# Sums of two attention masks moved from VectorE to GpSimd, two tiles ahead of their use

## What is computed

```python
qp = einsum(q, Wq) + bq ; kp = einsum(k, Wk) + bk
scores = qp @ kp.T * H ** -0.5 * layernorm(x)          # qc_score
mask = attn_mask[None, :, :] | key_padding_mask[:, None, :]
scores = where(mask, -inf, scores)
x = x + tanh(g_xattn) * softmax(scores)
h = layernorm(x)
logits = h @ gate_w.T ; w, sel = top_k(softmax(logits), 8)
x = x + tanh(g_ffn) * moe(h, sel, w, wg, wu, wd)
```

## Time and profile before

| | us |
|---|---|
| median of 3 runs | 1843.42 (1843.0 to 1848.21) |
| the profiled execution, its own time | 1842.44 |
| its span, from first to last instruction | 1840.7 |
| busy: PE, DVE, ACT, POOL | 1797.5, 1450.3, 1236.2, 1064.7 |

### The profile page before, as it was taken

How to read it: one execution, slowest core, us unless ns; L and a number is a source line. 1 busy time by engine, 2 the same in 40 slices (tenths; PEclk the granted TensorE clock), 3 DMA queues, 4 the chain that set the end, 5 groups by cost and what they waited for, 6 DMA issues and landing times.

```text
span 1840.7 us, 37183 instructions
## 1 busy us (share of the span) xinstructions
PE 1797.5 (98%) x13149; PEld 1316.9 (72%) x13149; DVE 1450.3 (79%) x2523; ACT 1236.2 (67%) x1806; POOL 1064.7 (58%) x817
## 2 busy tenths in 40 slices
PE   9999986999999999999999999999999999999997
PEld 4666655777777777777777777777777777777775
DVE  5999998777777777777777777777777777777772
ACT  6999986566666666666666666666666666666662
POOL 1000002776667666666666666677667766666651
PEclk9999997999999999999999999999999999999999
DMA  8677753799989999999999999999999999999982
GB/s 257 217 247 267 240 209 147 267 324 300 301 283 313 300 298 299 300 299 299 302 302 304 304 305 306 303 305 306 307 302 301 297 300 299 299 299 298 299 285 46
DMA packets 93849, 516.98 MB, mean 281 GB/s; under 512 B 17136, under 2 KB 19696, under 8 KB 69872
## 3 DMA queue, kind: packets, MB, share of 16 engines
q1 hardware_dynamic: 47056, 357.19, 49.3%
q0 software_dynamic: 43008, 151.04, 34.7%
q10 hardware_dynamic: 3744, 8.26, 1.6%
HBM read 409.21 MB, written 107.22 MB: 281 GB/s over the span
## 4 chain that ended last, share of the span: by engine, by line
PE 89%; DVE 5%; issue 2%; DMA 2%; ACT 1%; SPq 0%; POOL 0%; POOLq 0%; DVEq 0%; ACTq 0%
PE ps_gu L531 54%; PE ps_d L540 27%; PE ps_s L412 4%; PE ps_l L432 2%; PE ps_j L401 2%; DMA xb<-in_x 1%; DVE zb L898 1%; DVE zb L870 1%; PE ps_t L424 1%; DMA xg<-h_rows,g_idx 1%; DVE at L932 1%; PE ps_w L447 0%; DVE at L940 0%; ACT hT L645 0%; DVE hrow L960 0%
## 5 line engine op out<-in xcount | busy, mean ns | idle before, releaser
L1304 POOL DMA_INDIRECT xg<-h_rows,g_idx x504 | 724.5, 1437 | 187.9 <-issue 132.4
L531 PE MATMUL ps_gu<-xT,split_g 128*128 128x256 bf16 x4608 | 534.4, 273 | 0.7 <-DVE xT L1186 0.7
L531 PE MATMUL ps_gu<-xT,split_u 128*128 128x256 bf16 x4608 | 534.4, 273 | 0.0
L540 PE MATMUL ps_d<-split_d,act 128*128 128x512 bf16 x2304 | 507.9, 379 | 0.4 <-DVE act L1138 0.4
L531 PEld LDWEIGHTS ps_gu<-xT,split_g 128*128 128x128 bf16 x4608 | 450.8, 98 | 66.5 <-issue 0.9
L531 PEld LDWEIGHTS ps_gu<-xT,split_u 128*128 128x128 bf16 x4608 | 450.9, 98 | 52.2
L540 PEld LDWEIGHTS ps_d<-split_d,act 128*128 128x128 bf16 x2304 | 225.3, 98 | 259.1 <-DVE act L1138 1.2
L783 ACT ACTIVATE ob<-ps_d,wcol 128x512 f32<-128x512 f32 x256 | 173.1, 688 | 338.3 <-PE ps_d L540 338.3
L1324 POOL DMA_INDIRECT out<-ob,s_idx x128 | 205.4, 1604 | 294.2 <-ACT ob L783 202.5
L1146 DVE STREAM_TRANSPOSE xt<-xg 128x512 f32<-128x512 f32 x252 | 163.9, 689 | 151.2 <-DMA xg<-h_rows,g_idx 151.2
L1128 DVE TENSOR_TENSOR split_d<-raw_d,split_d 128x1536 bf16<-128x1536 f32 x128 | 219.3, 1753 | 73.1 <-ACT split_d L755 73.1
(11 more groups left out here) (116 smaller groups left out, 1402.3 us busy)
## 6 DMA issues: line engine op xcount, KB each, us to landing
raw_d<-in_wd SPq DMA_DIRECT2D x63, 1536.0 KB
raw_g<-in_wg SPq DMA_DIRECT2D x62, 1536.0 KB
raw_u<-in_wu SPq DMA_DIRECT2D x62, 1536.0 KB, 16.0
h_rows<-hrow SPq DMA_DIRECT2D x34, 640.0 KB, 3.4
xb<-in_x SPq DMA_DIRECT2D x32, 512.0 KB, 4.4
out<-xb SPq DMA_DIRECT2D x32, 512.0 KB, 3.2
xg<-h_rows,g_idx POOLq DMA_INDIRECT x512, 3.3
ctx_sb<-in_ctxT SPq DMA_DIRECT2D x8, 512.0 KB, 6.0
```

Source lines behind the costliest of these rows:

```text
L531: mm = pe.matmul(ps_gu[m][:, t, :], w[:, wi, k, m * P:(m + 1) * P], xT[u][:, k, xi, :], start=(k == 0 and (wi, xi) == (0, 0)), stop=(k == ...
L540: mm = pe.matmul(ps_d[n][:], act[u][:, ai, m, half * P:(half + 1) * P], split_d[:, wi, m, c * NH:(c + 1) * NH], start=(m == 0 and (wi, ai) ...
L1304: p.indirect_dma_start(out=xg[u][:, g, :], out_offset=None, in_=h_rows, in_offset=bass.IndirectOffsetOnAxis(ap=g_idx[u][:, g:g + 1].bitcas ...
```

## The change

`both` leaves VectorE's order and is issued by GpSimd. `both(0)`, `both(1)`, `both(2)` stand there behind the two first powers, and `both(g + 3)` behind `inverse_root(g)`. It waits for the pieces of the mask, for `kpm_used`, and for the `row_max` that last read its buffer (`z_ready`). The key mask's conversion stays on VectorE, where it now waits for the last sum of the batch before (`both_made`).

```diff
-            def both(g):
-
-                if g % TB == 0 and g:
-                    key_mask(g // TB)
-                v.wait_ge(kpm_used, g // TB + 1)
-                v.tensor_tensor(both_add[:, g % 2], mask_add[:, g % TB], kpm_add[:], ALU.add).then_inc(both_made, 1)
...
             v.wait_ge(mask_used, 2)
-            both(0)
-            both(1)
             minus_mean(1)
...
-            both(2)
...
                 step(picks, g - 1)
-                if g + 3 < N:
-                    both(g + 3)
+                if (g + 3) % TB == 0 and g + 3 < N:
+                    v.wait_ge(both_made, g + 3)
+                    key_mask((g + 3) // TB)
                 step(picks, g - 1)
                 minus_mean1(g)
...
+            def both(g):
+
+                p.wait_ge(mask_used, min(g % TB + 1, 2) if g < 2 else TB)
+                p.wait_ge(kpm_used, g // TB + 1)
+                if g >= 2:
+                    p.wait_ge(z_ready, g - 1)
+                p.tensor_tensor(both_add[:, g % 2], mask_add[:, g % TB], kpm_add[:], ALU.add).then_inc(both_made, 1)
...
+            for g in range(3):
+                both(g)
             for g in range(N):
                 inverse_root(g)
+                if g + 3 < N:
+                    both(g + 3)
```

## The result

The changed kernel takes 1882.5 us (median of 4 runs, 1879.52 to 1884.84) against 1844.04 before; the ratio is 1.0208, 95% interval 1.0195 to 1.0221. It is 38.5 us slower. The forecast was 1890 us in a range of 1841 to 1913, with slower as the likeliest outcome.

The account below looks back on a forecast made before the run. PE, DVE and ACT were taken as full together, DVE alone from 225 us on. 29 sums at +1.84 us give +53.4, less 8.2 absorbed, plus 1.5 at the start: +46.7 on 1842.4, median 1890 us, range 1841 to 1913.

Parts of the forecast that it names:

- The mechanism: At minus_mean1 on DVE: POOL's sum starts first and keeps the way into SBUF until it ends, a 2.3 us wait.
- The pass: Attention loop on DVE: 0.46 us saved, 2.3 us of block added, +1.84 us a pass, about 9.9 instead of 8.38.
- the wait for the power: Before minus_mean1: without the sum DVE arrives before POOL's power is ready, so 0.13 us of the gain becomes waiting.
- The sum's duration on POOL: 1024 columns, two inputs: 1.76 us plus 0.55 us, taken as 2.3 us; bounds 1.05 and 3.0 us.
- The absorbed idle time: Attention stage: DVE's existing idle time takes up 8.2 us of the 53.4 us that the loop's sums add.
- The start: First three sums, behind the second power on POOL: the path to the next power loses some 1.5 us.
- The ceiling: If DVE is not disturbed, 0.46 us a pass counts only in the last five or six passes: 2.8 us gained.
- The direction of the block: DVE and POOL at SBUF: whoever has started keeps the way until its instruction ends, the same in both directions.
- POOL does not give way: Denies the rival that DVE wins each time and POOL's sum stretches to 4 or 5 us: 1840 us, chance 0.19.
- The sharing case: Rival: the interface changes hands within an instruction, mainly slowing the 1.22 us comparison; 0.7 us a pass, 1855 us, chance 0.13.
- The lower clock: Rival: PE, busy about 84%, loses its full clock; half of 29 passes lose 1.5 us more, about 1912, chance 0.09.
- the slack: Passes at PE's lower clock, from 258 us on: 1.6 us of slack hides most of one such stretch.

Follow-up runs that it names:

- e6: Changed kernel with POOL summing only the first 512 columns and DVE the other 512; 1858.9 us.
- e4: Kernel before with no engine making the sum: the row maximum adds the attention mask alone; 1843.2 us, ratio 0.9984 to 1.0002.
- e8: Changed kernel with the first three sums back on DVE, the 29 of the loop on POOL; 1883.0 us.
- e5: As e1, with key moved behind x plus softmax and the tanh product's second factor a per-row scalar; 1858.0 us.
- e2: Changed kernel with POOL's sum replaced by a fill of the same buffer with zeros, reading nothing; 1848.6 us.
- e3: Changed kernel with nbias written as one tensor times a per-row scalar instead of a product of two tensors; 1877.8 us.
- e1: Changed kernel with POOL's sum waiting in addition for DVE's wide comparison of the same pass; 1856.9 us.
- e9: As e5, with the weights' product hrow put ahead of the wide comparison; 1846.3 us, ratio 1.0006 to 1.0024.

## Why the prediction was right

**The mechanism** is the one forecast, in the place forecast: POOL was first, and `minus_mean1` stood still for the rest of the sum.

**The pass.** Forecast: -0.59 for the sum, +0.13 for the wait for the power, +2.3 for the block, +1.84 us. Measured: 9.64 - 8.17 = +1.47, which is -0.59 + 0.13 + 1.93, with 2.07 - 0.14 = 1.93 us for the block. The term of 0.13 was right in size by luck, for it is not a wait for the power. The group of `nbias` shows 0.7 us of that in all 32 tiles. Most of it stands earlier, between the maximum and the load of its result, which the sum had filled (0.14 us from the maximum to the sum and 0.59 on to the load in the kernel before, 0.25 us here in all):

```profile
150.52 0.21 DVE L966 MAX8 top<-lg 128x8 f32<-128x64 f32 x1
150.77 0.09 DVE L969 MATCH_VALUE_LOAD left<-top,lg 128x8 f32 x1
```

**The sum's duration on POOL** was the term that was mis-sized: 2.12 instead of 2.3 us. I had added the whole 0.55 us of a short two-input instruction to the columns' 1.76. By the medians of e6 and of the changed kernel 512 columns cost 2.12 - 1.16 = 0.96 us, 1.9 ns a column, where I had 2 x 0.86 = 1.7, and what is left over is 0.2 us. The slope was about right and the fixed part too large. With the 0.14 us that the instruction takes anyway, which I did not subtract, the block was 0.37 us too long, 29 times: 10.7 us too much.

**The absorbed idle time** was too large, which made up for a part. Between the first power of the loop and that of g = 28 lie 28 passes, 28 x 1.47 = 41.2 us; the trace shows 271.7 against 234.7 us, +37.0, so 4.2 us were absorbed and not 8.2. In the first stretch DVE's busy time is 28.40 of 34: it idles there as before. The forecast went by DVE's idle time. By the numbers it was rather the difference between DVE's 8.17 us a pass and TensorE's 8.33 (e4): 9.64 - 8.33 = 1.31, and 28 x 1.31 = 36.7 us.

**The start** was 1.5 us in the sum and 0.8 in the trace, and cannot be told from nothing in the time (e8).

**The ceiling.** I had the greatest gain at 2.8 us, because only the last passes have DVE full alone. e4 shows no gain that can be measured; the interval reaches down to 0.9984, so up to some 3 us are not excluded. That part of the forecast, that the move could not pay even if it cost nothing, was right.

**The direction of the block** was taken to be symmetric from rows that showed only POOL waiting. e5 shows both directions in two neighbouring passes. What I had wrong is the list of what can be held: I counted instructions with two tensor inputs alone, and the one-tensor ones (`sel`, `hrow`) are held too (e2, e3, e5). Nothing in the forecast hung on it, but it cost e1 and e5 their expected times.

**The rivals.** POOL does not give way: its sum lasts 2.11 to 2.13 us in every pass of the changed kernel. The sharing case is out, since sharing would at most double the 0.14 us of `nbias`, and it waits to the sum's end. (The comparison keeps its 1.22 us, but it starts only after the sum, so it says nothing here.) The lower clock did not come on top: the mean granted clock is 1.00 in each stretch shown from 67 to 258 us, with PE busy 92% of the loop's middle (67.91 of 74 us) instead of all of it. From 286 to 315 us it is 0.83 to 0.88, and the passes stay at 9.64 us: the slack hides it, as the forecast said of one such stretch.

## What to carry to other kernels

Before you give POOL an elementwise instruction, look at what stands at that moment on DVE: a POOL instruction that reads SBUF for 2 us stops a DVE instruction of one column for 2 us, and the profile counts that as busy, so look at the means of short instructions, not at idle time. If it must be on POOL, let it start by a semaphore behind DVE's last two-input or one-tensor instruction and ahead of work from PSUM, with some distance. Here a margin of 0.1 us was a race, and any wait of DVE for another engine ate it up. And measure first what the engine gains when the work is left out altogether: here it was nothing.

## What the runs showed of the hardware

- DVE and POOL share two ways, and they block separately: POOL's write-only fill of 0.95 us left a two-tensor instruction at 0.16 us and stretched a one-tensor instruction of 64 columns to 0.83 us; POOL's copy and sum held the two-tensor instruction for 0.96 and 2.07 us.
- A one-column product with a per-row scalar is not held by the sum (0.21 us, e3), nor is a product of 1024 columns with an input in PSUM (1.28 us, e1); a one-column instruction with a constant is not held by the fill (0.14 us, e2).
- A POOL sum of two bf16 inputs takes 1.16 us for 512 columns and 2.12 for 1024.
- Moving one instruction of 0.35 us out of the sum's way was worth 12 us of 1858 (e5 against e9). It had been stretched nine times, to between 0.90 and 2.31 us, four times by arrivals less than 0.1 us apart and five times because DVE had waited for TensorE.
